# A per-image dynamic depthwise convolution: one order for all images, a later statistics chain, tap scaling on VectorE

## The reference, cut to what matters

```python
z = (x - mean(x)) / sqrt(var(x) + eps)              # per image and channel (32 groups of 1 channel)
avg = z.mean(axis=(2, 3))
wk = sigmoid(avg @ w1.T + b1).reshape(b * c, 1, 3, 3)
y = depthwise_conv(z, wk, padding=1) + conv_bias
out = x + (z - y) * fscale * z + y
```

## Time and profile before

| what | value |
|---|---|
| time, median of three runs | 283.49 us (282.74 to 284.69) |
| the profiled execution | 283.0 us |
| its span (first to last instruction) | 281.2 us |
| PE / PEld busy | 233.2 us (83%) / 167.4 us (60%) |
| DVE busy | 237.5 us (84%) |
| ACT busy | 213.3 us (76%) |
| POOL busy | 229.0 us (81%) |
| read and written in HBM | 39.31 MB and 37.75 MB, 274 GB/s over the span |
| chain that ended last, by engine | PE 41%, DVE 32%, waiting for nothing shown 15%, POOL 5%, DMA 4% |

### The profile page before, as it was taken

One profiled execution on the slowest core, in us unless ns is written; L12 is line 12 of the kernel. 1 busy time (PEld: TensorE's weight loads), 2 busy tenths in 40 slices (PEclk: granted clock), 3 DMA queues, 4 the chain that ended last, 5 costly groups with the idle time before them and its releaser, 6 DMA issues.

```text
span 281.2 us, 9000 instructions
## 1 busy us (share of the span) xinstructions
PE 233.2 (83%) x3506; PEld 167.4 (60%) x3506; DVE 237.5 (84%) x569; ACT 213.3 (76%) x386; POOL 229.0 (81%) x258
## 2 busy tenths in 40 slices
PE   0038985996989899898989898989899898999991
PEld 0024773784757576665656674757576665767660
DVE  2647787797999999999999999999999999766655
ACT  2126875787797979798898979797979799899520
POOL 0053448859899999999999999999999999999883
PEclk9999997797999999999999999999999999999997
DMA  7999803198496969798796969696969744444466
GB/s 266 334 411 420 347 11 128 43 350 335 151 364 266 359 265 373 282 320 366 252 418 232 402 252 371 261 367 262 370 259 373 303 170 171 171 171 170 168 256 252
DMA packets 10371, 77.64 MB, mean 276 GB/s; under 512 B 1265, under 2 KB 1496, under 8 KB 2648
## 3 DMA queue, kind: packets, MB, share of 16 engines
q1 hardware_dynamic: 10328, 77.06, 70.6%
HBM read 39.31 MB, written 37.75 MB: 274 GB/s over the span
## 4 chain that ended last, share of the span: by engine, by line
PE 41%; DVE 32%; issue 15%; POOL 5%; DMA 4%; SPq 1%; DVEq 0%; ACT 0%; POOLq 0%; ACTq 0%
PE conv_ps L426 26%; DVE outs L576 14%; PE conv_ps L432 9%; DVE pieces L523 8%; DMA gates<-gate 4%; DVE taps L543 4%; DVE row_stats L530 3%; PE dyn_ps L412 3%; POOL outs L841 2%; DVE less_one L535 2%; POOL inv_std L798 1%; PE conv_ps L488 1%; PE stat_ps L405 1%; DVE taps L550 1%; SPq L314 1%
## 5 line engine op out<-in xcount | busy, mean ns | idle before, releaser
L426 PE MATMUL conv_ps<-xs,taps 64*64 64x448 f32 x1536 | 223.4, 554 | 17.6 <-DVE outs L576 14.0
L841 POOL TENSOR_TENSOR outs<-outs,linear 128x1152 f32<-128x1152 f32 x63 | 166.2, 2645 | 9.1 <-DVE outs L576 9.1
L426 PEld LDWEIGHTS conv_ps<-xs,taps 64*64 64x64 f32 x1536 | 102.6, 135 | 61.9 <-issue 47.6
L576 DVE SCALAR_TENSOR_TENSOR outs<-xs,beta,conv_ps 128x576 f32<-128x576 f32 x128 | 102.6, 803 | 28.4 <-PE conv_ps L426 28.3
L432 PE MATMUL conv_ps<-xs,taps 64*64 64x128 f32 x1536 | 119.4, 279 | 0.0
L713 ACT ACTIVATE linear<-xs,slope 128x576 f32<-128x576 f32 x128 | 109.4, 858 | 3.6 <-POOL outs L841 3.6
L523 DVE BATCH_NORM_STATS2 pieces<-xs 128x6 f32<-128x64 f32 (+1 forms) x256 | 102.4, 449 | 5.3 <-DMA xs<-x 5.3
L688 ACT ACTIVATE xs<-xs,shift 128x594 f32<-128x594 f32 x128 | 99.5, 781 | 0.0
L432 PEld LDWEIGHTS conv_ps<-xs,taps 64*64 64x64 f32 x1536 | 94.1, 136 | 2.5 <-issue 1.8
L798 POOL TENSOR_TENSOR inv_std<-numbers,minus_half 128x8 f32<-128x8 f32 x16 | 26.4, 1650 | 4.5 <-ACT dev_mean L694 4.4
L543 DVE TENSOR_TENSOR taps<-dyn_ps,tap 128x1512 f32<-128x1512 f32 (+1 forms) x19 | 27.8, 1477 | 0.0
(11 more groups left out here) (59 smaller groups left out, 138.0 us busy)
## 6 DMA issues: line engine op xcount, KB each, us to landing
xs<-x SPq DMA_DIRECT2D x30, 1188.0 KB, 11.2
out<-outs SPq DMA_DIRECT2D x30, 1152.0 KB, 5.6
xs<-x SPq DMA_DIRECT2D x4, 594.0 KB, 5.9
out<-outs SPq DMA_DIRECT2D x3, 576.0 KB, 3.1
out<-outs SPq DMA_DIRECT2D x2, 288.0 KB, 2.6
cst<-const SPq DMA_DIRECT2D x1, 248.0 KB, 7.3
w1s<-w1r SPq DMA_DIRECT2D x1, 115.9 KB
gates<-gate SPq DMA_DIRECT2D x1, 8.0 KB
```

The costliest lines, as they stand in the source:

```text
L426: return nc.tensor.matmul(tile(i, g, taken)[:, START:BANK], taps[given, i % 2, at:at + HALF], xs[given, i % XBUFS, g, 0:PAIRED, 1 + shift: ...
L576: nc.vector.scalar_tensor_tensor(out=outs[:, i % OBUFS, g].rearrange("p (k w) -> p k w", w=COLS), in0=xs[:, i % XBUFS, g, :, 1:1 + COLS], ...
L841: nc.gpsimd.tensor_tensor(tile, tile, linear[:, PAIR * k:PAIR * (k + 1)].rearrange("p g n -> p (g n)"), ALU.add).then_inc(out_ready, 1)
```

## The change

It has five parts.

1. **One order for all images.** The places of images 0 and 1 go. VectorE has one order: product 0, 1, 2, aggregation (`rows`), product 3, `own_taps`, product 4, `matrices`, products 5 to 7, with one statistic behind each product. ScalarE's and TensorE's tables likewise.
2. **A later chain.** On TensorE the averages go from place 3 to 5, the dynamics from 5 and 6 to 7 and 8, the mean from 9 and 10 to 11 and 12, the sums of the moments from 13 and 14 to 15 and the next image's 0. On ScalarE the averages are copied ahead of group 4 instead of 3, the sigmoid stands ahead of group 6 instead of 5 and the counting moves from ahead of group 4 to behind the sigmoid. On GpSimd the moments stand behind pair add 1 instead of 0, the power and the columns of averages behind pair add 2 instead of 1.
3. **Taps scaled on VectorE**, in `own_taps`, straight behind the reduction; GpSimd's `scaled_taps` goes.
4. **Own-parity products moved.** `own_parity` of tile n-1 runs behind `across_first` of tile n, and `own_halves` becomes the last part of a tile.
5. **The start.** Image 1's sums of moments are made by a whole matmul ahead of the first tile, as are its means. The first image is loaded in eight pieces; the gate factors are loaded ahead of the constants, with a semaphore of their own; the weights' array is padded from 103 to 128 partitions; GpSimd waits for the reciprocal only ahead of `scales(0)`; the dummy matmuls read the first image's pieces.

The core of the diff (the start phases of VectorE and ScalarE and the semaphores are left out):

```diff
 TensorE, the table of chain(i, at):
-                    late = 3 if j <= 2 else 0
-                    if at == 3 + late:
+                    if at == 5:
                         averages(j)
-                    if at == 5 + late:
+                    if at == 7:
                         dynamics_first(j)
-                    if at == 6 + late:
+                    if at == 8:
                         dynamics_second(j)
...
+                    if at == 0 and j > 1:
+                        spread_odd(j)
                 j = i + 2
                 if j < B:
-                    if at == (11 if j == 2 else 9):
+                    if at == 11:
                         mean_even(j)
-                    if at == (12 if j == 2 else 10):
+                    if at == 12:
                         mean_odd(j)
-                    if at == (15 if j == 2 else 13):
+                    if at == 15:
                         spread_even(j)
...
                 across_first(i, g)
-                own_halves(i, g)
+                if n > 0:
+                    own_parity(*tiles[n - 1])
                 chain(i, 2 * g + 1)
                 across_second(i, g)
-                if n > 0:
-                    own_parity(*tiles[n - 1])
+                own_halves(i, g)
 VectorE, own_taps(j):
                 nc.vector.tensor_reduce(less_one[:], sig[:], AX_X, ALU.add).then_inc(less_one_ready, 1)
+                dve.wait_ge(roots_ready, j + 1)
+                dve.wait_ge(less_one_ready, j + 1)
+                nc.vector.tensor_tensor(tap[:], less_one[:].rearrange("p (g t) -> p g t", g=GROUPS),
+                                        roots[:, 1].unsqueeze(2).to_broadcast([PARTS, GROUPS, SETS]),
+                                        ALU.mult).then_inc(tap_ready, 1)
 ScalarE, the loop over the groups:
-                    if nxt and g == (4 if i < 2 else 3):
+                    if nxt and g == 1 and i > 0:
+                        copy_stats(i + 1)
+                    if nxt and g == 4:
                         copy_averages(i + 1)
-                    if stats and g == (5 if i == 0 else 4):
+                    if nxt and g == 6:
+                        sigmoid(i + 1)
+                    if stats and g == 6:
                         count(i + 2)
-                    if nxt and i > 1 and g == 5:
-                        sigmoid(i + 1)
...
 GpSimd, the loop over the images:
                 add_pair(i, 0)
-                if nxt and i > 1:
-                    scaled_taps(i + 1)
-                if stats and i > 0:
+                add_pair(i, 1)
+                if stats:
                     second_moments(i + 2)
-                if i < 2:
-                    scaled_taps(i + 1)
-                add_pair(i, 1)
...
-                if stats and i > 0:
+                add_pair(i, 2)
+                if stats:
                     deviation(i + 2)
                     average_columns(i + 2)
-                add_pair(i, 2)
...
 the start:
-            pool.wait_ge(params_loaded, 32)
+            pool.wait_ge(gates_loaded, 16)
...
-            pool.wait_ge(inv_ready, 1)
...
+            pool.wait_ge(inv_ready, 1)
             scales(0)
-            scaled_taps(0)
```

More of the change, by code:

```diff
@@ L482, in chain, with keep_warm @@
                         spread_even(j)
-                    if at == 14 and j > 2:
-                        spread_odd(j)
-            def keep_warm(count):
+            def keep_warm(weights, moving, count):
                 for _ in range(count):
-                    nc.tensor.matmul(conv_ps[:, CONV_TILES - 1, BANK:BANK + WARM], const_of("average")[0:HALF],
-                                     cst[0:HALF, 0:WARM], start=True, stop=True)
+                    nc.tensor.matmul(conv_ps[:, CONV_TILES - 1, BANK:BANK + WARM], weights, moving, start=True, stop=True)
@@ L491, in _ @@
+            first = xs[:, 0, 0].rearrange("p k w -> p (k w)")
+            pe.wait_ge(first_loaded[0], 16)
+            for g in range(GROUPS - 1):
+                at_least(pe, pieces_done, g)
+                keep_warm(first[:, 0:PARTS], first[:, 0:WARM], 1)
+            pe.wait_ge(consts_loaded, 16)
+            still = (const_of("average"), cst[:, 0:WARM])
             mean_whole(0)
+            keep_warm(*still, 1)
             spread_whole(0)
-            keep_warm(3)
+            keep_warm(*still, 4)
@@ L596, in _ @@
             nc.vector.tensor_copy(sig[:, :, SLOTS], const_of("centre")).then_inc(centres_filled, 1)
-            for g in range(GROUPS):
+            for g in range(2, GROUPS):
                 bn(1, g)
+            rows(1)
+            bn(2, 0)
             dve.wait_ge(centres_filled, 1)
             own_taps(0)
-            rows(1)
             first_matrices()
-            for g in range(START_AHEAD):
+            for g in range(1, START_AHEAD):
                 bn(2, g)
-            def bn_ahead(j, first, last):
-                if j < B:
-                    for g in range(first, last):
-                        bn(j, g)
+            ahead = [(j, g) for j in range(2, B) for g in range(GROUPS)][START_AHEAD:]
@@ new lines, in _ @@
+                product(i, 0)
+                bn_next(2 if i == 0 else 1)
+                product(i, 1)
+                bn_next(3 if i == 0 else 1)
+                product(i, 2)
+                bn_next()
+                if stats:
+                    rows(i + 2)
+                product(i, 3)
+                if nxt:
+                    own_taps(i + 1)
+                bn_next()
+                product(i, 4)
+                if nxt:
+                    matrices(i + 1)
+                bn_next()
@@ L661, in _ @@
+                product(i, 5)
+                bn_next()
+                product(i, 6)
+                bn_next()
+                if i == B - 1:
+                    add_last(GROUPS - 2)
+                product(i, 7)
+                bn_next()
             add_last(GROUPS - 1)
@@ L726, in _ @@
             copy_stats(0)
-            centre(0, 1)
-            centre(0, 2)
+            for g in range(1, 5):
+                centre(0, g)
             copy_averages(0)
-            centre(0, 3)
-            centre(0, 4)
+            count(1)
+            centre(0, 5)
             sigmoid(0)
-            count(1)
-            for g in range(5, GROUPS):
-                centre(0, g)
             negative_mean(1)
             fill_margins(1)
+            centre(0, 6)
+            copy_stats(1)
+            centre(0, 7)
             for i in range(B):
@@ L757, in _ @@
                         centre(i + 1, g)
[L758 to L763 removed]
+                if stats:
+                    negative_mean(i + 2)
+                    fill_margins(i + 2)
         @block.gpsimd
```

117 lines of the change are left out of this document (24 added, 93 removed).

## The result

| | before | after |
|---|---|---|
| time, median | 283.69 us (282.74 to 284.69, 4 runs) | 322.62 us (320.21 to 324.19, 4 runs) |
| ratio | | 1.1365 (95% interval 1.1283 to 1.1446) |
| profiled execution, its span | 283.0, 281.2 us | 322.49, 320.7 us |

The forecast was 318 us, in a range of 280 to 324. The page of the changed kernel: its first line, the busy times, and five groups of the costliest (busy, mean ns of one; then the idle time ahead of them and what ended it).

A forecast was written before the change was run, and what follows sets the result against it. The kernel was taken as bound by a ring of waits through VectorE and TensorE, 15.11 us per image. Image 0 to 43.6, thirteen images of 18.5, image 14 to 297.1, 19.4 to the end and 1.8 around: 318 us, range 280 to 324.

The forecast's parts named there:

- The ring: From the end of product 5 (p5) to the next image's, through averages, sigmoid, counting, aggregation and scaling: 18.5 us per image.
- The narrow step: On VectorE, the scaling is ready at 11.35 us, behind GpSimd's start of add 1 at 11.1: a margin of 0.25 us.
- The price of the scaling: On VectorE, the 72-column scaling takes 0.15 us itself and waits 2.3 us more for GpSimd's running pair add.
- Rival 1: The port is free, so the scaling does not wait for add 1: 16.2 us per image, 286 us (282 to 291); chance 0.22.
- The sum: Whole program: image 0 to 43.6 us, thirteen images of 18.5, image 14, the end, 1.8 around the span: 318 us.
- This last step: Image 14, without aggregation: scaling at 9.8 us waits into add 0, p5 ends about 14.5 us later, at 297.1.
- The start: Before the first product: gate factors loaded earlier give 4.9 us, image 1's matmuls and own-parity about 1; product at about 28.
- the late chain: GpSimd's power stands behind add 2, moving its part some 5 us; even with the cheapest scaling an image takes 16.2 us.
- the port: A VectorE instruction with two SBUF inputs is kept out while GpSimd's add runs: 2.3 us more for the scaling.
- rival 3: VectorE alone sets the pace, 14.75 us per image, 266 us; averages' columns needed 3.9 us after p5, not 5.06; chance 0.16.

The follow-up runs named there:

- the PSUM run: The changed kernel with the reduction writing its 72 numbers into PSUM, so the scaling has one operand in PSUM and one in SBUF: 288.94 us, ratio 1.0258.
- The run with both taken away: The changed kernel with GpSimd's power and columns of averages ahead of pair add 2 and the scaling's first operand in PSUM: 285.21 us, ratio 1.0127.
- the run with the earlier power: The changed kernel with GpSimd's power and columns of averages ahead of pair add 2 instead of behind it: 288.46 us, ratio 1.0261.

## Why the prediction was right, and where it was off

**The ring.** Its steps, from the end of p5 (138.06 + 0.79), against the image shown above:

| step | forecast | measured |
|---|---|---|
| columns of averages ready | 5.06 | 5.04 |
| copy of the averages starts | 5.7 | 5.65 |
| both groups done, sigmoid starts | 8.76 | 8.87 |
| aggregation starts, behind the counting | 9.5 | 9.61 |
| add 0 ends, add 1 follows | 11.1 | 11.08 |
| scaling starts | 11.35 | 11.54 |
| end of the next p5 | 18.5 | 18.43 |

Every edge that was named is in the trace, the wait for the averages (16.6 us over 12 images, 1.4 each, forecast about 1) and that for the counting included. The narrow step, whether the scaling comes before or after the start of add 1, was decided by 0.46 us where 0.25 had been forecast.

**The price of the scaling.** That the scaling waits out the running add was taken from a single pair of rows with another length; how long, 2.3 us beyond its own 0.15, from the places of the two in the ring. The row is 2.27, where about 2.4 had been forecast, since the scaling came 0.2 us later behind the start of add 1. That the mechanism is the one named, and not another, was open until the PSUM run. Rival 1, the same ring with the way free, was given 16.2 us and 286 us; that run has 16.40 and 288.94. Of the 0.2 us, half is the aggregation, which starts 9.61 and not 9.5 us after p5, and half is a hand-over that the sum left out: the scaling starts 0.63 us after the start of the reduction (118.28 to 118.91 in that run), where the reduction's length of 0.52 us had been taken. The scaling itself takes the 0.15 us that had been put on it (118.91 to the next statistic at 119.06).

**The sum.** Forecast 316.5 for the span, measured 320.7. The end of p5 of image 0: 43.6 against 43.98. Of image 13: 282.6 against 284.87, of which 2.7 are two images that took 19.75 us instead of 18.42 (below); that TensorE might lose its clock was named as a way in which the size could be wrong, but not priced. Of image 14: 14.5 us after it, measured 16.97. This last step is a mis-sized term: I took it that without an aggregation VectorE reaches the scaling at 9.8 us. But TensorE's late tile holds up p2 and p3 there too:

```profile
292.39 0.81 DVE L579 SCALAR_TENSOR_TENSOR outs<-xs,beta,conv_ps 128x576 f32<-128x576 f32 x1 [2.15 <-PE conv_ps L424]
294.57 0.81 DVE L579 SCALAR_TENSOR_TENSOR outs<-xs,beta,conv_ps 128x576 f32<-128x576 f32 x1 [1.36 <-PE conv_ps L424]
...
295.92 2.75 DVE L536 TENSOR_TENSOR tap<-less_one,roots 128x72 f32<-128x72 f32 x1
```

(VectorE's timeline of the changed kernel, image 14.) The scaling starts 11.05 us after the end of p5 and takes 2.75 us; it ends with add 1 and not with add 0.

**The start.** The first product came at 27.88 us, forecast 28. But the working was wrong in one place: the padding of the weights was taken as nothing, and the gate factors as 4.9 us. The runs give 2.2 us for the gate factors alone, and 3.4 for the padding on top of them; the padding without them was not run. That 28 us came out was luck: the padding, in the sum as nothing, made up what the gate factors could not give. Part 1 of the change and the rest of part 5 were not run alone.

**What the forecast did not see.** It held the late chain and the port for two steps of one ring, which they are, and rival 3 for a matter of 3.9 us at the averages. The run with both taken away stands at 16.16 us, on a third edge: GpSimd's moments, a pair add later, come directly ahead of the power that needs them back. This edge is hidden in the changed kernel, where add 2 stands between moments and power and GpSimd waits 4.07 us for p5 ahead of it anyway.

## What to carry to other kernels

Move a step of a chain only together with what it waits for and what waits for it: list for each engine what stands between two steps of the chain that make a round trip over other engines, and keep work between them. Before an instruction with two SBUF operands is moved from GpSimd to VectorE, look up what GpSimd does at the moment it will run; with one operand in PSUM it took 0.23 us beside a running add here. The part that gained (own-parity, 3% alone) was hidden under the parts that lost, so measure parts alone.

## What the runs showed of the hardware

- A VectorE instruction that waits for GpSimd's add goes through between two adds that follow each other without a gap, if it was waiting already: 0.54 us, in the run with the earlier power. In image 14 of the changed kernel it started at 295.92, just as add 0 ended and 0.01 us before the start of add 1 in GpSimd's timeline, and add 1 went first: 2.75 us.

```profile
295.94 2.65 POOL L809 TENSOR_TENSOR outs<-outs,linear 128x1152 f32<-128x1152 f32 x1
```

- TensorE's granted clock fell to 0.50, the lower of its two levels (1.2 GHz), in some images of the changed kernel and not in others, after nearly the same stand-still. It waited 1.98 us for p4, until 116.07 us, had 0.85 from 116 to 118 and 0.51 from 118.30 to 124.30, with a wait of 1.00 us for p5 in between. One image on it waited 2.09 us for p4 and 1.36 us for p5 (until 135.82 and 139.00) and kept 1.00. Where the low stretch lasts until the averages, TensorE comes to them 7.2 instead of 5.9 us after the start of p5, and the image takes 19.75 us. What decides it is open. The table of stretches of the changed kernel (columns as above):

```profile
118.30:124.30 6.00, 5.05 (x38) 3.23 (x42) 4.42 (x10) 4.64 (x8) 4.97 (x5) 0.51 0.63 255
...
136.00:138.00 2.00, 1.64 (x32) 1.15 (x27) 2.00 (x4) 0.11 (x1) 0.00 (x0) 1.00 1.02 399
138.00:140.00 2.00, 1.00 (x14) 0.64 (x18) 2.00 (x5) 2.00 (x5) 1.07 (x1) 1.00 0.97 410
```
